# Self-attention's maxima: two key halves in two row halves of the array, one wait for both

## The chip, the cores and the metric

The program runs on one core of one Trainium2 chip, in one launch. The metric is the device time of that core in microseconds (us): the median of several runs. The engines of a core run their own instruction streams and wait for each other on semaphores: TensorE (PE in the profile; PEld is its weight load), VectorE (DVE), ScalarE (ACT), GpSimd (POOL), and SyncE (SP), which here issues the transfers.

## The reference, cut to what matters

Two transformer layers run over two sequences of 1024 tokens with 256 features. Each layer is self-attention, attention over 77 context rows, and a gated feed-forward. The change is in self-attention alone:

```python
h = _layernorm(x, ln1_g, ln1_b)
q = (h @ wq).reshape(B, S, 16, 64);  k, v likewise
attn = jnp.einsum('bihd,bjhd->bhij', q, k) * 64 ** -0.5
attn = jax.nn.softmax(attn, axis=-1)
x = jnp.einsum('bhij,bjhd->bihd', attn, v).reshape(B, S, 1024) @ wo + bo + x
```

A softmax may subtract any number from a row of scores before its exponentials, if it is the same for the whole row. The kernel subtracts something near the row's largest score, so that no exponential overflows. That number needs no great precision.

## The kernel before, in words

**Precision.** A 32-bit number is held as two 16-bit parts, an upper and a lower one, and a product is made of three 16-bit products (upper by upper, upper by lower, lower by upper; `three`, lines 892 to 896). The queries and keys of a pair of heads are made on TensorE into one bank of PSUM. ScalarE copies the upper part out (L1331), VectorE takes the rest (L1533, a step called *take*), and SyncE then spreads the four staged parts over the tiles `qa`, `qb`, `ka` and `kb` of the two heads, head by head (L620). A head has 64 features, so a tile of 128 rows holds two things: `qa` has the upper part of the queries in both halves of its rows, `ka` the upper part of the keys in the head's own half (`mine`) and their lower part in the other (`others`).

**Rounds, pairs, heads, steps.** There are four rounds (two layers by two sequences). A round's self-attention walks eight pairs of heads, two heads to a pair, eight steps to a head: 4 x 8 x 2 x 8 = 512 steps. Every engine walks the same list of steps, which `self_unit` writes out, and does its share of each; nothing reorders an engine's queue. TensorE's share of a step is, in this order:

1. the first key half of one tile of *maxima* (L980): 128 queries by 512 keys into PSUM, for the head that comes next;
2. what is *placed* in this step for the next pair: a projection of queries (`q`, two steps), of keys (`k`, two) or of values (`v`, two); or a `merge` (two, transposes), or one of the three small products for the context (`ck`, `cm`, `cv`). Some steps have none;
3. `score`: the scores of 512 queries and 256 keys (L997, L1004), for two exponentials of ScalarE (L1373, L1374);
4. the second key half of the tile of maxima (L980 again);
5. `value`: probabilities by values of an earlier step, 24 short products (L1022 to L1026).

VectorE's share is, in this order: the reduction of the first half of the maxima (L1574), the take of what was placed (L1533 for `q` and `k`, L1539 `v`, L1545 `merge`, L1549, L1555, L1564), the reduction of the second half, and then, where it falls to VectorE and not to GpSimd, the lower part of an earlier step's probabilities (*refine*, L1585), and at two steps of each head a reciprocal and a product (*gather*, L1591 and L1593).

**Counts.** In a round, 28 of the 128 steps have a projection of queries or keys placed and 14 one of values (seven pairs have a next one), 14 have a merge, and 8 each have `ck`, `cm` and `cv`. Over the four rounds that is 112, 56, 56, 32, 32 and 32; the other 192 steps have nothing placed. In the first pair of a round some steps hold two tiles of maxima, since that pair's own are not all made yet.

**The banks.** The maxima have two banks of PSUM, `work[0]` and `work[2]`, used in turn (`PEAK_RING` is 2). VectorE's reduction frees one by counting up `peak_free`, which starts at 2. `next_peak` makes product number n wait for n + 1, so for the reduction of number n - 2: a first half waits for the first half of the tile before it, a second half for the second.

Of the kernel before, what the change touches and what calls it, by code (L numbers as in the profile page):

```python
# [10 lines left out]
F16 = mybir.dt.float16  # L11
# [3 lines left out]
P = 128  # L15
# [3 lines left out]
HEADS, DH = 16, 64  # L19
# [8 lines left out]
BLK = 512  # L28
# [7 lines left out]
HALF = TILES // 2  # L36
# [94 lines left out]
PEAK = ("max",)  # L131
# [17 lines left out]

FIRST_POLISHED = (0, 1, 2, 3, 4, 5, 6)  # L150
SCORE_RING, PEAK_RING, HIGH_RING = 2, 2, 1
MOVES = 12


def queries(par, ahead):
# [220 lines left out]
def build(nc, io):  # L376
    ctx = ExitStack()
    with ctx:
        def sb(name, shape, dtype=F32):
            return ctx.enter_context(nc.sbuf_tensor(name, shape, dtype))  # L380
# [4 lines left out]
        def sem(name):  # L385
            return ctx.enter_context(nc.semaphore(name))
# [5 lines left out]
        self_peaks = [work[0], work[2]]  # L392
# [26 lines left out]
        xn = sb("xn", [P, 4, DIM])  # L419
# [21 lines left out]
        qa = [[sb(f"qa{p}{i}", [P, TOKENS], F16) for i in range(2)] for p in range(2)]  # L441
        qb = [[sb(f"qb{p}{i}", [P, TOKENS], F16) for i in range(2)] for p in range(2)]
        ka = [[sb(f"ka{p}{i}", [P, TOKENS], F16) for i in range(2)] for p in range(2)]
        kb = [[sb(f"kb{p}{i}", [P, TOKENS], F16) for i in range(2)] for p in range(2)]
        vals = [sb(f"vals{p}", [P, TILES, 2, VW], F16) for p in range(2)]
        prob32 = sb("prob32", [P, 4, TOKENS])
        prob = [sb(f"prob{i}", [P, 4, TOKENS], F16) for i in range(2)]
# [22 lines left out]
        def moves(which, par, head):  # L470

            mine, others = [slice(r, r + DH) for r in (head * DH, (1 - head) * DH)]
            up, low = [part[mine, :] for part in staged["qk".index(which)]]
            qa_, qb_, ka_, kb_ = [t[par][head] for t in (qa, qb, ka, kb)]
            if which == "q":
                return [(qa_[mine, :], up), (qa_[others, :], up), (qb_[mine, :], low)]
            return [(ka_[mine, :], up), (ka_[others, :], low), (kb_[mine, :], up)]

        def o_half(s):

# [49 lines left out]
        a = collections.namedtuple("Sems", names)(*[sem(f"self_{n}") for n in names.split()])  # L530
# [357 lines left out]
        def _(pe):  # L888
# [9 lines left out]
            def attention(g):  # L898
                pace = Pace(g)
                b = g % BATCH  # L900

                def bank():

                    n = pace.here(*HIGH)
                    if n >= len(first_high):
                        pe.wait_ge(a.work_free, pace.n(*HIGH) + HIGH_RING)
                    elif n >= 4:
                        pe.wait_ge(a.work_free, pace.n(*HIGH) - 3 + HIGH_RING)
                    elif n == 2 and g:

                        pe.wait_ge(inner_ready, g * (BLKS * FF_CHUNKS) + 2)
                    return high_bank(n)

                def next_peak():

                    pe.wait_ge(a.peak_free, pace.n(*PEAK) + 1)
                    return self_peaks[pace.here(*PEAK) % PEAK_RING]

                def weight(kind, c, column):
                    return [wp[kind][:, part, column + (c if column == 0 else 2 * c), :] for part in range(2)]  # L920

                def do(step, pair):
                    par, head, s = step.par, step.head, step.step
# [3 lines left out]
                    elif step.kind in ("q", "k"):  # L927
# [3 lines left out]
                        out = bank()  # L931
# [5 lines left out]
                    elif step.kind == "v":  # L937
                        out = bank()
# [7 lines left out]
                    elif step.kind == "ck":  # L946

                        pe.wait_ge(cross_split, pace.n("ck") + 1)
                        out = bank()
# [4 lines left out]
                    elif step.kind == "cm":  # L954

                        out = bank()
# [4 lines left out]
                    elif step.kind == "cv":  # L961
                        out = bank()
# [7 lines left out]
                    elif step.kind == "arrive":  # L970

                        pe.wait_ge(a.head0_ready, pace.n("arrive", times=8 * MOVES) + (8 * MOVES + CREDIT))
                    elif step.kind == "max":
                        if head == 1 and s == (0, 0):

                            pe.wait_ge(a.head1_ready, pace.n("arrive", times=8 * MOVES) + CREDIT)
                        out = next_peak()
                        t, h = s
                        first_query = t // HALF * BLK + t % HALF
                        pe.matmul(out[:, :], qa[par][head][:, first_query:first_query + (P - 1) * HALF + 1:HALF],  # L980
                                  ka[par][head][:, h * BLK:(h + 1) * BLK], start=True, stop=True)\
                            .then_inc(a.peak_full, 1)
                    elif step.kind == "score":
                        if pace.here("score") == 0:

# [6 lines left out]
                        out = scores[pace.here("score") % SCORE_RING]  # L992
# [3 lines left out]
                        for keys, at in parts:  # L996
                            pe.matmul(out[:, at], ka[par][head][:, keys], qa[par][head][:, q],  # L997
                                      start=True, stop=False)
# [8 lines left out]
                    elif step.kind == "value":  # L1007
# [7 lines left out]
                        for i, k in enumerate([2 * (s % KEY_STEPS) + i for i in range(2)]):  # L1015
                            v = vals[par][:, k, head, :]
                            for t in range(HALF):
                                out = self_outs[:, t * OUT_W:(t + 1) * OUT_W]
# [4 lines left out]
                                          stop=False, skip_group_check=True)  # L1023
# [3 lines left out]
                                                 stop=(k == TILES - 1), skip_group_check=True)  # L1027
                        last.then_inc(a.probs_used, 1)
                    elif step.kind == "merge":
                        out = bank()  # L1030
# [281 lines left out]
        def _(act):  # L1312
            act.sem_inc(a.exp_done, SCORE_RING)

            def attention(g):
# [7 lines left out]
                def do(step, pair):  # L1323
                    par, head, s = step.par, step.head, step.step
                    if step.kind == "start":

                        act.wait_ge(a.head0_ready, pace.pairs(8 * MOVES) + CREDIT)
                        act.wait_ge(a.head1_ready, pace.pairs(8 * MOVES) + CREDIT)
                    elif step.kind in ("q", "k"):
# [153 lines left out]
            for dest, source in moves("k", 0, 0):  # L1483
                act.dma_start(dest, source).then_inc(a.head0_ready, 16)
# [412 lines left out]
```

## Time and profile before

| what | us |
|---|---|
| median of 3 runs (2157.67 to 2160.73) | 2160.64 |
| the profiled execution, its own time | 2162.83 |
| its span, from the first to the last instruction | 2161.1 |

The span is what the profile's rows add up to; about 1.7 us lie around it. Busy time is the time in which an engine has at least one instruction under way. Matmuls are pipelined: one of 512 columns has a duration of 0.38 us, but the next one starts 0.22 us after it, so the distance of two starts tells what a matmul costs and not its duration.

### The profile page before, as it was taken

To read this page: it belongs to the slowest core of one execution; us is meant where nothing else is said; L and a number is where in the kernel's file an instruction comes from. 1 tells how busy PE (TensorE), PEld (TensorE's weight loads), DVE (VectorE), ACT (ScalarE), POOL (GpSimd) and SP (SyncE) were. 2 spreads that over 40 slices of the span, in tenths; PEclk is the share of its full clock that TensorE was granted. 3 is DMA by queue.
4 is the path that set the end of the run, shared out by engine and by line. 5 is a ranking of instruction groups with operands and counts; after the bars stand their busy time and mean duration, and the time that the engine had idled before them with its cause. 6 is when DMAs were issued, how large, how long until landed. Compare 5 with 4: busy or idle time off the path is not lost.

```text
span 2161.1 us, 58920 instructions
## 1 busy us (share of the span) xinstructions
PE 2087.5 (97%) x25120; PEld 1413.0 (65%) x25120; DVE 1618.5 (75%) x3014; ACT 1473.5 (68%) x1950; POOL 1375.3 (64%) x860
## 2 busy tenths in 40 slices
PE   6999999999999999999999999999999999999999
PEld 2666666775666666668466666676746666667675
DVE  6888887657688888765768888866577888885664
ACT  4888889345488888834548888874455888886442
POOL 6878887353378887835347887773424888775540
PEclk8999999999999999999999999999999999999999
DMA  4322220040332232004032233100403323210120
GB/s 137 77 56 65 72 73 19 11 96 26 77 92 65 56 84 61 19 16 99 25 94 75 65 77 77 45 29 9 97 21 90 85 72 83 56 39 21 23 62 20
DMA packets 134245, 127.82 MB, mean 59 GB/s; under 512 B 83424, under 2 KB 95712, under 8 KB 133984
## 3 DMA queue, kind: packets, MB, share of 16 engines
q1 hardware_dynamic: 133744, 123.67, 23.0%
q8 instruction: 198, 3.24, 0.6%
q14 instruction: 63, 0.52, 0.1%
q10 hardware_dynamic: 240, 0.39, 0.1%
HBM read 55.72 MB, written 4.19 MB: 28 GB/s over the span
## 4 chain that ended last, share of the span: by engine, by line
PE 74%; DVE 9%; ACT 5%; POOL 4%; issue 4%; DMA 2%; SPq 1%; POOLq 1%; DVEq 0%; ACTq 0%
PE work L980 10%; PE scores L1004 9%; PE scores L997 9%; PE scores L894 5%; PE scores L896 5%; PE scores L895 5%; PE work L1026 5%; PE work L1022 5%; PE work L1024 5%; PE work L894 4%; PE work L896 4%; PE work L895 4%; DVE minima L1574 2%; ACT prob L1374 1%; PE work L1034 1%
## 5 line engine op out<-in xcount | busy, mean ns | idle before, releaser
L830 POOL TENSOR_TENSOR prob<-prob 128x1024 f16<-128x1024 f32 x328 | 709.4, 2179 | 290.1 <-ACT prob L1374 274.4
L1574 DVE TENSOR_REDUCE minima<-work 128x1 f32<-128x512 f32 x1024 | 681.7, 683 | 53.3 <-PE work L980 47.2
L1373 ACT ACTIVATE prob<-scores 128x1024 f32<-128x1024 f32 x512 | 526.3, 1028 | 94.8 <-PE scores L1004 75.1
L1374 ACT ACTIVATE prob<-scores 128x1024 f16<-128x1024 f32 x512 | 522.8, 1021 | 0.0
L1022 PE MATMUL work<-vals,prob 128*128 128x65 f16 x4096 | 428.8, 192 | 2.2 <-POOL prob L830 1.8
L1026 PE MATMUL work<-vals,prob 128*128 128x65 f16 x4096 | 429.4, 195 | 0.0
L1024 PE MATMUL work<-vals,prob 128*128 128x64 f16 x4096 | 429.2, 193 | 0.0
L1022 PEld LDWEIGHTS work<-vals,prob 128*128 128x128 f16 x4096 | 383.0, 99 | 66.1 <-issue 17.9
L1024 PEld LDWEIGHTS work<-vals,prob 128*128 128x128 f16 x4096 | 379.8, 97 | 52.8
L980 PE MATMUL work<-ka,qa 128*128 128x512 f16 x1024 | 390.2, 384 | 24.6 <-DVE minima L1574 19.2
L1026 PEld LDWEIGHTS work<-vals,prob 128*128 128x128 f16 x4096 | 380.2, 97 | 0.0
L1004 PE MATMUL scores<-qb,kb 128*128 128x512 f16 (+1 forms) x1024 | 305.5, 379 | 0.0
L997 PE MATMUL scores<-qa,ka 128*128 128x512 f16 x1024 | 305.1, 380 | 0.3
L1585 DVE TENSOR_TENSOR prob<-prob 128x1024 f16<-128x1024 f32 x184 | 247.9, 1347 | 15.2 <-ACT prob L1374 15.2
L894 PE MATMUL scores<-wide,oT 128*128 128x256 f16 x768 | 210.9, 275 | 0.9 <-issue 0.5
L895 PE MATMUL scores<-wide,oT 128*128 128x256 f16 x768 | 211.0, 275 | 0.0
L896 PE MATMUL scores<-wide,oT 128*128 128x256 f16 x768 | 210.9, 275 | 0.0
L980 PEld LDWEIGHTS work<-ka,qa 128*128 128x128 f16 x1024 | 115.8, 113 | 107.0 <-DVE minima L1574 37.6
L1004 PEld LDWEIGHTS scores<-qb,kb 128*128 128x128 f16 (+1 forms) x1024 | 100.6, 98 | 121.2 <-issue 0.6
L894 PE MATMUL scores<-hT,wide 128*128 128x512 f16 (+1 forms) x416 | 158.9, 382 | 3.8 <-DVE prob L1780 3.6
L895 PE MATMUL scores<-hT,wide 128*128 128x512 f16 (+1 forms) x416 | 157.7, 379 | 0.0
L896 PE MATMUL scores<-hT,wide 128*128 128x512 f16 (+1 forms) x416 | 157.7, 379 | 0.0
(168 smaller groups left out, 4161.3 us busy)
## 6 DMA issues: line engine op xcount, KB each, us to landing
qa<-staged_q SPq DMA_DIRECT2D x128, 128.0 KB, 2.3
ka<-staged_k SPq DMA_DIRECT2D x126, 128.0 KB, 2.3
raw_even<-in_pairs SPq DMA_DIRECT2D x32, 384.0 KB, 3.4
raw_odd<-in_pairs SPq DMA_DIRECT2D x32, 384.0 KB, 3.4
raw_odd<-in_pieces SPq DMA_DIRECT2D x20, 512.0 KB, 3.4
raw_even<-in_pieces SPq DMA_DIRECT2D x20, 512.0 KB, 3.5
qb<-staged_q SPq DMA_DIRECT2D x64, 128.0 KB, 2.3
kb<-staged_k SPq DMA_DIRECT2D x63, 128.0 KB, 2.3
```

Source lines behind the costliest of these rows:

```text
L830: pool.tensor_tensor(prob[1][:, slot, :], prob32[:, slot, :], prob[0][:, slot, :], ALU.subtract).then_inc(a.polished, 1)
L894: pe.matmul(out, left[0], right[0], start=first, stop=False)
L895: pe.matmul(out, left[0], right[1], start=False, stop=False)
L896: return pe.matmul(out, left[1], right[0], start=False, stop=last)
L980: pe.matmul(out[:, :], qa[par][head][:, first_query:first_query + (P - 1) * HALF + 1:HALF], ka[par][head][:, h * BLK:(h + 1) * BLK], start ...
L1004: last = pe.matmul(out[:, at], kb[par][head][rows_, keys], qb[par][head][rows_, q], start=False, stop=True)
L1022: pe.matmul(out, p_hi, v[:, DH:VW], start=(first and i == 0 and t == 0), stop=False, skip_group_check=True)
L1024: pe.matmul(out[:, 0:DH], p_hi, v[:, 0:DH], start=False, stop=False, skip_group_check=True)
L1026: last = pe.matmul(out, p_lo, v[:, DH:VW], start=False, stop=(k == TILES - 1), skip_group_check=True)
L1373: act.activation(prob32[:, n % RING, :], source, ACT.Exp)
L1374: act.activation(prob[0][:, n % RING, :], source, ACT.Exp)\
L1574: dve.tensor_reduce(minima[:, t, h:h + 1], out[:, :], AX.X, ALU.max, negate=True)\
```

## The change

The two halves of a tile of maxima are multiplied in one place, where the first half stood, and from upper parts alone. The first half uses the 64 rows `mine` of `qa` and `ka`; the second uses the 64 rows `others` of `qa` (the same upper queries) and of a new tile `km`, which holds the upper part of the second 512 keys in those rows. Both wait once, for `n + 2`. `km` lies in the memory of `xn` and is filled by one more transfer for each head and pair (`MOVES` counts 14 in place of 12). In the steps' list nothing is moved: VectorE's two reductions stay where they are.

```diff
-MOVES = 12
+MOVES = 14
...
+        km = [xn[:, p, :].bitcast(F16) for p in range(2)]
...
-            return [(ka_[mine, :], up), (ka_[others, :], low), (kb_[mine, :], up)]
+            return [(ka_[mine, :], up), (km[par][others, :], up[:, BLK:2 * BLK]), (ka_[others, :], low),
+                    (kb_[mine, :], up)]
...
-                def next_peak():
-
-                    pe.wait_ge(a.peak_free, pace.n(*PEAK) + 1)
-                    return self_peaks[pace.here(*PEAK) % PEAK_RING]
-
...
-                        out = next_peak()
                         t, h = s
+                        if h:
+                            return
+                        n = pace.here(*PEAK)
+                        mine, others = [slice(r, r + DH) for r in (head * DH, (1 - head) * DH)]
                         first_query = t // HALF * BLK + t % HALF
-                        pe.matmul(out[:, :], qa[par][head][:, first_query:first_query + (P - 1) * HALF + 1:HALF],
-                                  ka[par][head][:, h * BLK:(h + 1) * BLK], start=True, stop=True)\
-                            .then_inc(a.peak_full, 1)
+                        queries_ = slice(first_query, first_query + (P - 1) * HALF + 1, HALF)
+
+                        pe.wait_ge(a.peak_free, pace.n(*PEAK) + 2)
+                        pe.matmul(self_peaks[n % PEAK_RING][:, :], qa[par][head][mine, queries_],
+                                  ka[par][head][mine, 0:BLK], start=True, stop=True).then_inc(a.peak_full, 1)
+                        pe.matmul(self_peaks[(n + 1) % PEAK_RING][:, :], qa[par][head][others, queries_],
+                                  km[par][others, :], start=True, stop=True).then_inc(a.peak_full, 1)
```

On TensorE, in a step of the first pair with a projection of queries placed (L894 to L896; `work0` and `work2` are the banks of the maxima, `scores0` the step's scores, `work3` the values), the row before is:

```order
L980 MATMUL work0<-ka11,qa11 128x512 [waits self_peak_free]
L894 MATMUL work1<-hT0,wpS 128x512 [waits self_work_free]
L895 MATMUL work1<-hT1,wpS 128x512
L896 MATMUL work1<-hT0,wpS 128x512
...
L997 MATMUL scores0<-qa10,ka10 128x512 [waits self_exp_done]
...
L1004 MATMUL scores0<-qb10,kb10 128x512 x2
L980 MATMUL work2<-ka11,qa11 128x512 [waits self_peak_free]
L1022 MATMUL work3<-vals0,prob0 128x65 [waits self_polished]
```

and now, with the line numbers of the changed kernel (L983 and L985 are the two halves, L896 to L898 the projection, L1001 and L1008 the scores, L1026 the values):

```order
L983 MATMUL work0<-ka11,qa11 128x512 [waits self_peak_free]
L985 MATMUL work2<-xn,qa11 128x512
L896 MATMUL work1<-hT0,wpS 128x512 [waits self_work_free]
L897 MATMUL work1<-hT1,wpS 128x512
L898 MATMUL work1<-hT0,wpS 128x512
...
L1001 MATMUL scores0<-qa10,ka10 128x512 [waits self_exp_done]
...
L1008 MATMUL scores0<-qb10,kb10 128x512 x2
L1026 MATMUL work3<-vals0,prob0 128x65 [waits self_polished]
```

The second half has moved from behind the scores to right behind the first, and its wait has gone into the first one's.

On VectorE, around a take of keys (L1537) and one of `ck` (L1553) in the first pair, the changed kernel's order is the following; before, the same rows stand in the same order, four line numbers lower:

```order
L1578 TENSOR_REDUCE minima<-work0 128x1 [waits self_peak_full]
L1537 SCALAR_TENSOR_TENSOR staged_k1<-work1,staged_k0 128x512 [waits self_work_high]
L1578 TENSOR_REDUCE minima<-work2 128x1 [waits self_peak_full]
L1578 TENSOR_REDUCE minima<-work0 128x1 [waits self_peak_full]
L1553 SCALAR_TENSOR_TENSOR kd1<-work1,kd0 64x77 [waits self_work_high]
```

Nothing moved here: the reduction of `work2` stands behind the take.

On SyncE, in the first spread of keys, the row before is:

```order
L643 DMA qb01<-shift160 1x128x4
L620 DMA ka10<-staged_k0 64x1024
L620 DMA ka10<-staged_k1 64x1024
L620 DMA kb10<-staged_k0 64x1024
L620 DMA ka11<-staged_k0 64x1024
```

and now:

```order
L645 DMA qb01<-shift160 1x128x4
L622 DMA ka10<-staged_k0 64x1024
L622 DMA xn<-staged_k0 64x512
L622 DMA ka10<-staged_k1 64x1024
L622 DMA kb10<-staged_k0 64x1024
L622 DMA ka11<-staged_k0 64x1024
```

One transfer more stands in each head's share, ahead of the other head's.

## Rows read from the trace of the kernel before

**Rows 1.** The page, part 1: busy us (share of the span) and instructions.
```profile
PE 2087.5 (97%) x25120; PEld 1413.0 (65%) x25120; DVE 1618.5 (75%) x3014; ACT 1473.5 (68%) x1950; POOL 1375.3 (64%) x860
```

**Rows 2.** Self-attention of round one: length, busy of PE, PEld, DVE, ACT, POOL; clock.
```profile
41.00:378.00 337.00, 330.73 (x4478) 219.06 (x4477) 280.65 (x487) 287.11 (x357) 264.86 (x140) 1.00 0.24 62
```

**Rows 3.** Groups by line (page, part 5): busy us, mean ns, idle before, its releaser.
```profile
L980 PE MATMUL work<-ka,qa 128*128 128x512 f16 x1024 | 390.2, 384 | 24.6 <-DVE minima L1574 19.2
```

**Rows 4.** Timeline of PE, a step with a projection of queries: start us, duration us.
```profile
666.70 0.38 PE L980 MATMUL work<-ka,qa 128*128 128x512 f16 x1
666.92 0.38 PE L894 MATMUL work<-hT,wpS 128*128 128x512 f16 x1
...
668.21 0.59 PE L997 MATMUL scores<-qa,ka 128*128 128x512 f16 x2
...
669.08 0.38 PE L980 MATMUL work<-ka,qa 128*128 128x512 f16 x1
...
670.04 0.38 PE L980 MATMUL work<-ka,qa 128*128 128x512 f16 x1
```

**Rows 5.** Timeline of ACT and DVE in the same step: copy, take, second reduction.
```profile
668.41 0.60 ACT L1331 ACTIVATE staged_q<-work 128x512 f16<-128x512 f32 x1 [0.54 <-PE work L896]
...
669.04 0.69 DVE L1533 SCALAR_TENSOR_TENSOR staged_q<-work,staged_q 128x512 f16<-128x512 f32 x1 [1.23 <-ACT staged_q L1331]
669.65 0.68 DVE L1574 TENSOR_REDUCE minima<-work 128x1 f32<-128x512 f32 x1
```

**Rows 6.** Timeline of DVE and PE where PE waits for a reduction.
```profile
318.89 0.68 DVE L1574 TENSOR_REDUCE minima<-work 128x1 f32<-128x512 f32 x1
...
319.62 0.41 PE L980 MATMUL work<-ka,qa 128*128 128x512 f16 x1 [0.66 <-DVE minima L1574]
```

**Rows 7.** Timeline of PE around the eight transposes with 8 weight columns.
```profile
435.03 0.38 PE L896 MATMUL scores<-hT,wide 128*124 128x512 f16 x1
435.34 0.61 PE L1107 MATMUL work<-ident,x_shift 128*8 128x128 f16 x8
435.88 0.43 PE L894 MATMUL scores<-hT,wide 128*124 128x512 f16 x1
436.15 0.38 PE L895 MATMUL scores<-hT,wide 128*124 128x512 f16 x1
```

**Rows 8.** Groups by line: the take of values.
```profile
L1539 DVE SCALAR_TENSOR_TENSOR vals<-work,vals 128x512 f16<-128x512 f32 x64 | 44.3, 694 | 41.3 <-ACT vals L1339 41.3
```

**Rows 9.** Timeline, a step with a merge: PE's tile, its second reduction, the next tile.
```profile
658.73 0.38 PE L980 MATMUL work<-ka,qa 128*128 128x512 f16 x1
...
661.04 0.68 DVE L1574 TENSOR_REDUCE minima<-work 128x1 f32<-128x512 f32 x1
...
661.21 0.38 PE L980 MATMUL work<-ka,qa 128*128 128x512 f16 x1
```

**Rows 10.** Timeline, a step with `cm`: the same three.
```profile
683.02 0.38 PE L980 MATMUL work<-ka,qa 128*128 128x512 f16 x1
...
684.94 0.68 DVE L1574 TENSOR_REDUCE minima<-work 128x1 f32<-128x512 f32 x1
...
685.45 0.38 PE L980 MATMUL work<-ka,qa 128*128 128x512 f16 x1
```

**Rows 11.** Timeline, a step with nothing placed: two tiles' starts, two reductions at once, one alone.
```profile
673.38 0.38 PE L980 MATMUL work<-ka,qa 128*128 128x512 f16 x1
...
674.33 1.28 DVE L1574 TENSOR_REDUCE minima<-work 128x1 f32<-128x512 f32 x2
...
675.41 0.38 PE L980 MATMUL work<-ka,qa 128*128 128x512 f16 x1
...
675.82 0.69 DVE L1574 TENSOR_REDUCE minima<-work 128x1 f32<-128x512 f32 x1 [0.22 <-PE work L980]
```

**Rows 12.** Timeline, VectorE's refine, and SyncE issuing two transfers of keys.
```profile
670.25 1.39 DVE L1585 TENSOR_TENSOR prob<-prob 128x1024 f16<-128x1024 f32 x1
...
680.33 1.24 SPq L620 DMA_DIRECT2D ka<-staged_k  x2
```

## The prediction

> **What bounds the kernel now.** I read the busy shares first: TensorE is busy 97% of the span, the others 75% or less [rows 1]; in the first round's self-attention, 337 us long, TensorE has 331 us, ScalarE 287, VectorE 281 and GpSimd 265, at a granted clock of 1.00, the 2.4 GHz level [rows 2]. So TensorE is the bound and three engines stand close behind it. Then the groups by line: the 1024 products of maxima waited 24.6 us in all [rows 3], so before the change the reductions hardly ever hold TensorE up. Then the timeline of one step with a projection of queries, which the rest is built on [rows 4]. Products start 0.22 us after each other (666.70 to 666.92). The step runs from 666.70 to the next tile's first half at 670.04, 3.34 us without a hole: 0.22 the first half, 1.29 the projection (666.92 to 668.21), 0.87 the scores (to 669.08), 0.96 the second half and the values.
>
> The timeline of ScalarE and VectorE beside it decides this case [rows 5]. ScalarE copies the projection from 668.41, VectorE's take follows at 669.04, and only behind the take comes the second reduction, 669.65 to 670.33. The next tile has by then been started at 670.04, 0.29 us earlier. That is allowed now, because a first half waits for the first reduction alone.
>
> **What goes and what comes.** The pair of products costs 0.43 us a tile now. Two at once would cost one product and a small shift. With 512 tiles that is the gain to be had: 512 x (0.43 - 0.24) = 97 us, if nothing else came.
>
> *The switch between whole rows and half rows.* No row before shows a product of 64 rows. The nearest rows are the eight transposes with 8 weight columns, which use another part of the array than their neighbours [rows 7]. Ahead of them the next start is due at 435.03 + 0.22 = 435.25 and comes at 435.34: 0.09 us lost. Behind them, eight starts 0.055 us apart end at 435.78 and the next comes at 435.88: 0.10 lost, and its weight load, which could not be made beforehand, costs 0.05 more (436.15 - 435.88 is 0.27, not 0.22). With 128 weight columns the uncovered load is 0.03: where TensorE waited for a reduction, the product's duration is 0.41 and not 0.38 [rows 6]. The price of a switch is thus between 0 (a product can't start before the one ahead has been fed in, so it gains nothing) and 0.15 us; I take 0.09 each way with 0.03 for a load, the rows' own value. A tile then costs 0.09 + 0.03 (first load) + 0.03 (second load, by which the second half starts later) + 0.21 + 0.09 + 0.03 = 0.48 us against 0.43, so by itself the change loses 0.05 x 512 = 28 us. The Trainium skill has a rule for this in "TensorEngine Tiling (Array Packing)", Key Properties: changing the tiling mode, not just the tile, drains the engine. Those transposes agree with it at 0.09 us; for 64 rows no run here shows it.
>
> *The wait.* It is the dearer part. Both halves now wait for both reductions of the tile before, and the second of them stands behind the take in VectorE's queue. So in a step with something placed a ring closes: tile, projection, copy, take, second reduction, next tile. Nothing behind the waiting product on TensorE (projection, scores, values) can go ahead. Its length for a projection: from the end of the second reduction to the next product 0.05 (318.89 + 0.68 = 319.57, then 319.62 [rows 6]); loads 0.06; the product 0.21; the switch back with a load 0.12. That makes 0.44 to the projection's start; the switch on entry is hidden in the wait. From there the trace has 666.92 to 670.33, 3.41. The ring is 3.85 us against 3.34: 0.51 a step. Put for any step: from the first half's start to the end of the second reduction, less 0.22, plus 0.44.
>
> - Projections of queries and keys 112, of values 56 (their take lasts 0.69 too [rows 8]): 168 x 0.51 = 86.
> - Merges: 658.73 to 661.72 is 2.99, plus 0.22 makes 3.21, against 2.48 now (661.21) [rows 9]: 0.73 x 56 = 41.
> - `cm`: 683.02 to 685.62 is 2.60, makes 2.82 against 2.43 [rows 10]: 0.39 x 32 = 12.
> - `ck` and `cv` are of the same build with two and three small pieces to a take: I set them between the last two, 0.56 x 64 = 36.
> - Nothing placed, 192 steps. A step takes 2.03 (673.38 to 675.41). After a reduction's end VectorE needs 0.05 + 0.03 + 0.41 (from a product's start to its reduction, 675.41 to 675.82) + 1.28 for two reductions in a row [rows 11] = 1.77, less than TensorE's 2.03 + 0.05, so the switch alone counts. But where a refine, 1.39 us [rows 12], comes first (by the list of steps about one such step in five), the two reductions end some 0.45 later than TensorE's own work. 0.8 x 0.05 + 0.2 x 0.45 = 0.13; x 192 = 25.
> - The first pair's steps that carry two tiles pass the ring with two more reductions behind the take: three to a round, about 0.5 more each, 6.
> - The transfers: SyncE issues two in 1.24 us [rows 12], so each head's keys arrive 0.64 us later. Within a round steps with slack follow the spread; at a round's start, where TensorE comes directly to the maxima, 0.64 x 4 = 3.
>
> What hides the rest: the exponentials, 2.05 us a step, get more room, since steps become longer. The lower parts left out of the maxima change the shift a little and no time. The sum is 86 + 41 + 12 + 36 + 25 + 6 + 3 = 209. The profiled execution took 2162.8 (span 2161.1 and 1.7 around it), 2.2 above the median of the runs. 2162.8 + 209 = 2372, against the median 2370.
>
> **Rivals.**
>
> *The halves one after the other.* The two products have their own weights, rows and banks, but no row here shows two at once. Run in turn, a tile costs 0.21 - 0.03 = 0.18 more, in the ring too: 512 x 0.18 = 92, so 2462.
>
> *The ring stays open, the switch is paid.* If the second reduction ended before TensorE comes back (a quicker copy and take, VectorE being otherwise free), only 28 us remain: 2188. Against it: copy, take and reduction follow each other within 0.04 us in the step shown [rows 5]; nothing in them waits for anything that the change speeds up.
>
> *Faster.* The place is the 512 tiles, the price 0.19 us each, the mechanism two products in the time of one. It decides if a switch costs under 0.06 us both ways together and the reductions are done when TensorE comes back. Both would give 2161 - 97 = 2064 at most; ScalarE, at 287 of 337 us [rows 2], still fits. For it: TensorE's share and the unbroken pitch of 0.22. Against it: the 0.29 us by which the second reduction is already late, and rows 7. With free switches and the ring as it stands, the ring is still 3.76 against 3.34. The Trainium skill's "TensorE: Matmul & The Clock Gate", Part 3, The mechanism, states that products in different row groups overlap, their starts about 4 ns apart. By that rule alone the time is this rival's; the trace has no such pair.
>
> **How the numbers follow.** The ring with halves at once 0.83, halves in turn 0.07, open ring with switches 0.05, faster 0.04, no change (a switch that costs just what the overlap gives, open ring) 0.01. The likeliest is the first: 2370. Its own bounds are the switch's: with none, 320 steps with something placed lose 0.09 less (29) and 192 others up to 0.26 less (50), so 2291; with 0.05 more for every load's exposure on the way out, 512 x 0.02 to 0.04, 2390. Upwards the range has to reach the halves in turn, 2462. So 2290 to 2465. About 0.2%, 4 us, is what a measurement can tell from no change. Faster 0.04, same 0.01, slower 0.95.
>
> **What would show it.** In the profile after: waits of the first half (L983) for VectorE's reductions near 200 us in place of 25; TensorE's share near 85%; a step with a projection near 3.85 us and a merge near 3.2; the second half (L985) starting about 0.03 us after the first, and the next product about 0.3 after that. A start 0.21 later would show halves in turn; a next product 0.22 after the second half would show a free switch. I am wrong at the root if the first half finds both reductions done in steps with a projection, so that those steps stay at 3.34 or fall below.

## The result, and the profile after

The changed kernel took 2335.95 us (median of four runs, 2332.85 to 2338.72) against 2159.66 for the kernel before (2157.67 to 2160.73): a ratio of 1.0816, 95% interval 1.0799 to 1.0833. It is 176 us slower; 2370 was forecast, in a range of 2290 to 2465. The profiled execution took 2334.5, with a span of 2332.8.

Part 1 of the page after, in the form of [rows 1]:

```profile
PE 2108.8 (90%) x25120; PEld 1388.7 (60%) x25120; DVE 1644.1 (70%) x3014; ACT 1480.5 (63%) x1950; POOL 1350.6 (58%) x860
```

Nearly the same busy time lies in a span that is 172 us longer; every engine's share has fallen. The first round's self-attention, to set against [rows 2]:

```profile
42.40:421.80 379.40, 336.79 (x4478) 214.40 (x4477) 286.21 (x486) 288.74 (x357) 258.36 (x140) 0.99 0.23 57
```

It takes 379.4 us in place of 337.0, at a mean granted clock of 0.99 in place of 1.00 (for this 0.01 see "The rest" below). TensorE is busy for 337 us of it, so it now stands still for over 40. For what, the groups by line tell (L983 and L985 are the two halves, L1578 their reduction), to set against [rows 3]:

```profile
L1578 DVE TENSOR_REDUCE minima<-work 128x1 f32<-128x512 f32 x1024 | 681.3, 683 | 116.0 <-PE work L985 114.2
...
L983 PE MATMUL work<-ka,qa 64*128 64x512 f16 x512 | 207.8, 406 | 180.3 <-DVE minima L1578 173.2
...
L985 PE MATMUL work<-xn,qa 64*128 64x512 f16 x512 | 208.7, 408 | 0.0
```

The first half waited 173 us for reductions, where 19 were waited before; the second half never waits. And the reductions in turn waited 114 us for L985: that is the mark of a ring, two engines that wait for each other by turns. Part 4 of the page, the chain that ended last, first before, then after:

```profile
PE 74%; DVE 9%; ACT 5%; POOL 4%; issue 4%; DMA 2%; SPq 1%; POOLq 1%; DVEq 0%; ACTq 0%
```

```profile
PE 43%; DVE 32%; ACT 11%; issue 7%; POOL 4%; DMA 1%; POOLq 1%; SPq 0%; ACTq 0%; DVEq 0%
```

TensorE set the end for three quarters of the time; now VectorE and ScalarE set it for 43%.

One step with a projection of queries shows the ring. The timeline of PE, to set against [rows 4] (start us, duration us; in brackets the idle time before and its releaser):

```profile
722.25 0.41 PE L983 MATMUL work<-ka,qa 64*128 64x512 f16 x1 [0.62 <-DVE minima L1578]
722.25 0.40 PE L985 MATMUL work<-xn,qa 64*128 64x512 f16 x1
722.59 0.39 PE L896 MATMUL work<-hT,wpS 128*128 128x512 f16 x1
722.82 0.38 PE L897 MATMUL work<-hT,wpS 128*128 128x512 f16 x1
...
726.07 0.40 PE L983 MATMUL work<-ka,qa 64*128 64x512 f16 x1 [0.41 <-DVE minima L1578]
```

Its weight loads:

```profile
722.25 0.11 PEld L983 LDWEIGHTS work<-ka,qa 64*128 64x128 f16 x1 [0.74 <-DVE minima L1578]
722.25 0.11 PEld L985 LDWEIGHTS work<-xn,qa 64*128 64x128 f16 x1
722.59 0.10 PEld L896 LDWEIGHTS work<-hT,wpS 128*128 128x128 f16 x1 [0.23 <-issue]
```

And ScalarE's copy, VectorE's take and second reduction, to set against [rows 5]:

```profile
724.09 0.60 ACT L1335 ACTIVATE staged_q<-work 128x512 f16<-128x512 f32 x1 [1.24 <-PE work L898]
...
724.72 0.69 DVE L1537 SCALAR_TENSOR_TENSOR staged_q<-work,staged_q 128x512 f16<-128x512 f32 x1 [1.34 <-ACT staged_q L1335]
725.33 0.68 DVE L1578 TENSOR_REDUCE minima<-work 128x1 f32<-128x512 f32 x1
```

The two halves truly run at once: both products start at 722.25 and both loads too (3 ns apart in the trace's nanoseconds). The next product comes 0.34 later. But the second reduction ends at 725.33 + 0.68 = 726.01, and only then, at 726.07, may the next tile start: the step is 3.82 us and was 3.34. Copy, take and reduction follow each other without a hole, VectorE having stood idle for 1.34 before the take.

All steps, from one tile's first product to the next one's (medians; loss is the sum of all differences to before; the first steps of a round and the steps between rounds apart):

| step | number | before | after | loss, us |
|---|---|---|---|---|
| projection q, k | 100 | 3.340 | 3.821 | 56.5 |
| projection v | 56 | 3.387 | 3.874 | 27.2 |
| merge | 48 | 2.476 | 3.094 | 27.6 |
| `ck` | 28 | 2.242 | 2.851 | 10.3 |
| `cm` | 28 | 2.429 | 2.796 | 10.5 |
| `cv` | 28 | 2.767 | 3.354 | 16.2 |
| nothing placed | 156 | 2.076 | 2.052 | 3.0 |
| first steps of rounds | 48 | 1.727 | 1.902 | 12.9 |

With 1.5 in the last steps of rounds and between rounds that is 166 of the span's 172. The other 5.6 lie in four intervals that the table leaves out, one a round: behind the last step that holds two tiles, the next tile waits for a second reduction that stands behind VectorE's gather (L1595, L1597), 2.67 us where it was 1.25. Of the 100 steps with q or k, 98 start the next tile within 0.08 us of the second reduction's end; before the change none had to.

### The profile page after: what moved, and what is told of

Its sections match the earlier page's. It is cut to its first block, busy times and chain, and to the rows that moved or that the text cites. A ratio compares the mean times of both kernels' runs of the same rounds, so it can differ in the third digit from the quotient of the medians.

```text
span 2332.8 us, 58984 instructions
## 1 busy us (share of the span) xinstructions
PE 2108.8 (90%) x25120; PEld 1388.7 (60%) x25120; DVE 1644.1 (70%) x3014; ACT 1480.5 (63%) x1950; POOL 1350.6 (58%) x860
## 4 chain that ended last, share of the span: by engine, by line
PE 43%; DVE 32%; ACT 11%; issue 7%; POOL 4%; DMA 1%; POOLq 1%; SPq 0%; ACTq 0%; DVEq 0%
DVE minima L1578 14%; PE work L983 6%; DVE prob L1589 6%; PE scores L896 5%; PE scores L898 5%; PE scores L897 5%; PE work L896 4%; PE work L898 4%; PE work L897 3%; PE scores L1001 3%; PE scores L1008 2%; ACT prob L1377 2%; ACT prob L1378 2%; DVE vals L1543 2%; DVE staged_q L1537 2%
## 5 line engine op out<-in xcount | busy, mean ns | idle before, releaser
L832 POOL TENSOR_TENSOR prob<-prob 128x1024 f16<-128x1024 f32 x328 | 724.2, 2213 | 470.1 <-ACT prob L1378 462.6
L1578 DVE TENSOR_REDUCE minima<-work 128x1 f32<-128x512 f32 x1024 | 681.3, 683 | 116.0 <-PE work L985 114.2
L1026 PE MATMUL work<-vals,prob 128*128 128x65 f16 x4096 | 431.6, 193 | 0.4
L1026 PEld LDWEIGHTS work<-vals,prob 128*128 128x128 f16 x4096 | 383.3, 99 | 63.5 <-issue 6.0
L983 PE MATMUL work<-ka,qa 64*128 64x512 f16 x512 | 207.8, 406 | 180.3 <-DVE minima L1578 173.2
L1001 PE MATMUL scores<-qa,ka 128*128 128x512 f16 x1024 | 309.1, 384 | 0.5
L1008 PE MATMUL scores<-qb,kb 128*128 128x512 f16 (+1 forms) x1024 | 306.2, 380 | 0.0
L1589 DVE TENSOR_TENSOR prob<-prob 128x1024 f16<-128x1024 f32 x184 | 268.0, 1456 | 15.0 <-ACT prob L1378 15.0
L896 PE MATMUL scores<-wide,oT 128*128 128x256 f16 x768 | 209.4, 273 | 0.8 <-issue 0.8
L898 PE MATMUL scores<-wide,oT 128*128 128x256 f16 x768 | 209.3, 273 | 0.0
L985 PE MATMUL work<-xn,qa 64*128 64x512 f16 x512 | 208.7, 408 | 0.0
L983 PEld LDWEIGHTS work<-ka,qa 64*128 64x128 f16 x512 | 56.0, 109 | 245.6 <-DVE minima L1578 197.3
L1008 PEld LDWEIGHTS scores<-qb,kb 128*128 128x128 f16 (+1 forms) x1024 | 101.1, 99 | 122.7 <-issue 3.0
L896 PE MATMUL scores<-hT,wide 128*128 128x512 f16 (+1 forms) x416 | 158.9, 382 | 3.8 <-DVE prob L1784 3.6
L897 PE MATMUL scores<-hT,wide 128*128 128x512 f16 (+1 forms) x416 | 157.7, 379 | 0.0
```

Of the source, the lines that this page charges most:

```text
L832: pool.tensor_tensor(prob[1][:, slot, :], prob32[:, slot, :], prob[0][:, slot, :], ALU.subtract).then_inc(a.polished, 1)
L896: pe.matmul(out, left[0], right[0], start=first, stop=False)
L897: pe.matmul(out, left[0], right[1], start=False, stop=False)
L898: return pe.matmul(out, left[1], right[0], start=False, stop=last)
L1008: last = pe.matmul(out[:, at], kb[par][head][rows_, keys], qb[par][head][rows_, q], start=False, stop=True)
L1026: pe.matmul(out, p_hi, v[:, DH:VW], start=(first and i == 0 and t == 0), stop=False, skip_group_check=True)
```

## The experiments

Each ran on the chip beside the kernel before, which took 2159.5 to 2161.7 us there; ratios have their 95% intervals.

**Both reductions ahead of the take.** The list of steps gives VectorE the second reduction directly behind the first; on TensorE nothing is moved.

```diff
-        out += [step for step in peaks_of[s] if step.kind == "arrive"] + peaks[:1]
+        out += [step for step in peaks_of[s] if step.kind == "arrive"] + peaks[:2]
...
-        spread = [peaks[1:2], peaks[2:3], peaks[3:]] if len(peaks) > 2 else [[], peaks[1:], []]
+        spread = [[], peaks[2:], []]
```

> The changed kernel with one edit in the list of steps: VectorE's second reduction stands ahead of the take of what is placed, right behind the first reduction. Theory (ring: the next tile waits for a second reduction that stands behind the take): the ring opens, a tile then costs 0.447 us on TensorE (0.098 in, 0.004, 0.336 to the next product, 0.011) against 0.432 before, so 2161 + 0.015 x 512 = 2168; bounds 2150 to 2185. Rival (the switch to half rows and back is what costs): nothing of that is changed, so about 2336.

Measured: 2206.29 (2203.35 to 2209.97), ratio 1.0215 (1.0198 to 1.0232). Timeline of PE, then of DVE, in a step with a projection of queries:

```profile
680.64 0.41 PE L983 MATMUL work<-ka,qa 64*128 64x512 f16 x1
...
683.99 0.40 PE L983 MATMUL work<-ka,qa 64*128 64x512 f16 x1
```

```profile
681.09 1.29 DVE L1578 TENSOR_REDUCE minima<-work 128x1 f32<-128x512 f32 x2 [0.55 <-PE work L985]
683.12 0.69 DVE L1537 SCALAR_TENSOR_TENSOR staged_q<-work,staged_q 128x512 f16<-128x512 f32 x1 [0.74 <-ACT staged_q L1335]
```

The reductions are through at 682.38, 1.6 us before the next tile needs their banks. The step is 3.35 long, and no projection step waits any more. So at least 130 of the 176 us were the ring through VectorE's queue (the new order costs something itself, as the third experiment shows). The time is 21 above the upper bound I had set: of the 46 us left, the first steps of rounds have 13, nothing placed 8, merges 6.5, `cv` 6, `ck` 4, projections 2.5, and the four intervals left out above 2.5. In half of the merges VectorE has a refine of the step before in front of the two reductions:

```profile
710.27 1.71 DVE L1589 TENSOR_TENSOR prob<-prob 128x1024 f16<-128x1024 f32 x1
711.90 1.27 DVE L1578 TENSOR_REDUCE minima<-work 128x1 f32<-128x512 f32 x2
```

That step's tile starts at 710.52 and the next at 713.23, 0.06 after the reductions' end (711.90 + 1.27 = 713.17): a short ring in place of the long one.

**Whole rows, one wait.** The kernel before, with its 128-row products, both halves in one place behind one wait for n + 2; 12 transfers as before.

```diff
-                        out = next_peak()
...
+                        if h:
+                            return
+                        n = pace.here(*PEAK)
...
+                        pe.wait_ge(a.peak_free, pace.n(*PEAK) + 2)
+                        for i in range(2):
+                            pe.matmul(self_peaks[(n + i) % PEAK_RING][:, :], qa[par][head][:, queries_],
+                                      ka[par][head][:, i * BLK:(i + 1) * BLK], start=True, stop=True)\
+                                .then_inc(a.peak_full, 1)
```

> The kernel before with both halves in one place and one wait for both reductions, but with products over all 128 rows as before and without the new tile or its transfer; VectorE's order as in both kernels. Theory (ring): the ring stays closed and holds 0.432 + 0.03 for the two products in place of 0.346 + 0.011, so 0.1 more in about 320 steps: 2336 + 33 = 2369; bounds 2345 to 2385. Rival (switch): without half rows the time goes back to about 2161.

Measured: 2349.02 (2348.24 to 2350.02), ratio 1.0876 (1.0859 to 1.0892). PE and DVE in a step with a projection:

```profile
721.60 0.60 PE L986 MATMUL work<-ka,qa 128*128 128x512 f16 x2
722.03 0.38 PE L894 MATMUL work<-hT,wpS 128*128 128x512 f16 x1
...
725.58 0.41 PE L986 MATMUL work<-ka,qa 128*128 128x512 f16 x1 [0.48 <-DVE minima L1580]
```

```profile
724.85 0.68 DVE L1580 TENSOR_REDUCE minima<-work 128x1 f32<-128x512 f32 x1
```

With no half rows at all nearly the whole loss is there, with the same wait for the second reduction (725.53 to 725.58). So the switch of the array's form is not needed for the loss. The half rows even make the ring shorter, by 0.11 a projection step (3.929 here).

**Whole rows, both reductions ahead of the take.** The edit of the first experiment on the kernel before.

> The kernel before with both halves in one place (each with its own wait, all 128 rows) and both reductions ahead of the take. Theory (ring): no ring, TensorE streams as before: 2145 to 2165, and the difference from the same order with half rows is the net price of halves at once, some 7 us in favour of whole rows (0.015 x 512). Rival (switch): 2161 too; it would put the difference from half rows at 170 or more.

Measured: 2179.95 (2179.02 to 2181.10), ratio 1.0093 (1.0078 to 1.0108): a miss by 15. Of its 20 us the `cv` steps have 12 (median 3.260, before 2.767); projections stay at 3.34. The order by itself is not free. What makes `cv` long stands in the waits of the weight loads, first before, then here:

```profile
PEld work L894 <- DVE oT L1545: 4.9, 5, 1.1
```

```profile
PEld work L894 <- DVE oT L1545: 15.8, 28, 1.1
```

What is placed has one bank, which the take (here a merge's, L1545) frees; the take now stands behind a refine and both reductions, and the next placed product waits for it. The order opens one ring and closes another, shorter one.

The half rows cost 26 beyond it (2206 to 2180), where I had expected about 7: 5 of them are the transfers (next). The other 21 were not taken apart; they hold the switch, and a fall of the clock in the first pair (see "The rest" below).

**The transfers alone.** The kernel before with `km` and its two transfers a pair, never read.

```diff
-MOVES = 12
+MOVES = 14
...
+        km = [xn[:, p, :].bitcast(F16) for p in range(2)]
```

> The kernel before with the new tile and its transfers alone (14 moves a pair; the tile is filled and never read). Theory (ring): the transfers are covered but for a round's start: 0 to 5 us more than before, 2161 to 2166. Rival (the transfers cost a good part of the loss, through SyncE's queue): 2180 or more.

Measured: 2164.61 (ten runs, 2162.33 to 2168.14), ratio 1.0023 (1.0014 to 1.0033): 5 us. The weight loads' waits for the keys' transfers doubled, from 6.3 us, 6 times, to:

```profile
PEld work L982 <- DMA kb<-staged_k: 13.1, 12, 5.2
```

**Half rows, each in its old place with its own wait.** Two stays in half rows a tile, and nothing at once.

```diff
-                        if h:
-                            return
...
+                        rows_, keys_ = (others, km[par][others, :]) if h else (mine, ka[par][head][mine, 0:BLK])
-                        pe.wait_ge(a.peak_free, pace.n(*PEAK) + 2)
+                        pe.wait_ge(a.peak_free, pace.n(*PEAK) + 1)
```

> The changed kernel's products (64 rows, upper parts, the new tile and its transfer) in the old places and with the old waits: each half by itself, the second behind the scores. Theory (ring for the time lost, and a switch that the overlap just pays): the ring is open again, but each half now pays the way in and out by itself, 0.098 + 0.336 + 0.011 = 0.445 us against 0.216, so 2161 + 5 for the transfers + 0.23 x 1024 = 2400; some of it falls into waits that TensorE has anyway: 2370 to 2405. Rival (half rows cost nothing to enter and leave; only the shared wait costs): 2165.

Measured: 2359.24 (2358.92 to 2369.12) against 2161.65, ratio 1.0929 (1.0905 to 1.0953). The waits of weight loads, and where the load could not go ahead (us, times, longest):

```profile
PEld work L982 <- issue: 147.8, 349, 1.1
PEld work L1023 <- issue: 107.7, 470, 0.6
...
PEld work L982 <- DVE minima L1575: 87.3, 190, 1.3
```

Here the switch can be priced by itself: from the last whole-row product to the first of half rows 0.10 us is lost, on the way back 0.12 (sums over the pairs of lines at the values, L1027 to L982 less a pitch of 0.030, and L982 to L1023 less 0.216: 45.9 us in 460, 55.9 us in 464). A step with nothing placed has two stays and takes 2.48 in place of 2.08. So with each half by itself the kernel loses 198 us, more than the changed kernel's 176; part of that is waits for reductions (87.3 above, 37.6 at L980 before). The time is 11 below my bounds and 41 below the 2400 of the working; that this part of the switch fell into waits that TensorE has anyway, as the expectation put it, was not measured.

**Both halves in the same 64 rows**, one after the other behind the common wait (`MOVES` 12).

```diff
-                        pe.matmul(self_peaks[(n + 1) % PEAK_RING][:, :], qa[par][head][others, queries_],
-                                  km[par][others, :], start=True, stop=True).then_inc(a.peak_full, 1)
+                        pe.matmul(self_peaks[(n + 1) % PEAK_RING][:, :], qa[par][head][mine, queries_],
+                                  ka[par][head][mine, BLK:2 * BLK], start=True, stop=True).then_inc(a.peak_full, 1)
```

> The changed kernel with the second half multiplied in the same 64 rows as the first (the head's own rows of the keys), so that the two cannot run at once; without the new tile and its transfers, else the same. Theory (the two halves run at once and that is worth one product's 0.213 us in every tile, in the ring too): 2336 - 5 + 0.213 x 512 = 2440; bounds 2420 to 2450. Rival (they do not really run at once; the records of their starts mislead): 2331, as the changed kernel without its transfers.

Measured: 2426.09 (2421.18 to 2427.62), ratio 1.1224 (1.1207 to 1.1241). PE at a tile:

```profile
762.75 0.40 PE L983 MATMUL work<-ka,qa 64*128 64x512 f16 x1 [0.40 <-DVE minima L1578]
762.99 0.38 PE L985 MATMUL work<-ka,qa 64*128 64x512 f16 x1
763.30 0.39 PE L1001 MATMUL scores<-qa,ka 128*128 128x512 f16 x1
```

The second half starts 0.24 later and the next product 0.55 after the first, in place of 0.34. Different rows are what lets the halves run at once, and that is worth 90 us here.

**The wait split.** The first half waits for n + 1, the second for n + 2.

```diff
-                        pe.wait_ge(a.peak_free, pace.n(*PEAK) + 2)
+                        pe.wait_ge(a.peak_free, pace.n(*PEAK) + 1)
...
+                        pe.wait_ge(a.peak_free, pace.n(*PEAK) + 2)
```

> The changed kernel with the wait parted: the first half waits for the first reduction of the tile before, the second half, right behind it, for the second. Theory (what counts is where the second reduction stands on VectorE, behind the take): TensorE stands at the second half in place of the first, the ring stays closed: 2336, bounds 2320 to 2350. Rival (the single wait of both halves is the fault): back to about 2165 to 2200.

Measured: 2323.01 (2322.64 to 2326.64), ratio 1.0754 (1.0738 to 1.0770). The wait has moved to the second half (L986):

```profile
PEld work L986 <- DVE minima L1579: 138.5, 348, 1.3
```

Counted from one second half to the next, the steps are as long as in the changed kernel: 3.817 us with `q` or `k` placed and 3.871 with `v`, for 3.821 and 3.874 (medians). It is not the common wait by itself that costs, but that the second half stands ahead of the placed work: what stands behind it on TensorE can't pass.

**The refines moved.** Three tries to give the first experiment, or the kernel before, other steps in which VectorE makes the lower parts (`POLISHED`, the steps of each head that go to GpSimd): in the first no refine stands ahead of a merge's reductions any more; in the other two only the second heads of a pair change. VectorE makes what the list does not name: in first heads of a pair 0, 3 and 7 (the expectation below says 1, 3 and 7), in second heads 0, 2 and 6.

```diff
-POLISHED = ((1, 2, 4, 5, 6), (1, 3, 4, 5, 7))
+POLISHED = ((1, 3, 4, 5, 6), (0, 2, 3, 4, 5))
```

> The kernel with both reductions ahead of the take (2206), with VectorE's three refines of a head moved to steps that a projection follows: steps 1, 3 and 7 done by VectorE in even heads become 0, 2 and 7, those of odd heads 1, 6 and 7. Theory (what is left there is a refine of 1.2 to 1.5 us between a tile and its reductions where the next step is short: merge 0.23, cv 0.26, a step with nothing placed 0.12): 18 less, 2188; bounds 2175 to 2200. Rival (what is left is the price of half rows): 2206.

Measured: 2229.19 (2225.25 to 2233.25), ratio 1.0316 (1.0295 to 1.0337). A miss: merges wait no more, but the projections of queries and keys lost 37 us, since VectorE comes late behind two refines in a row (the second step with `q` takes 0.72 us longer).

```diff
-POLISHED = ((1, 2, 4, 5, 6), (1, 3, 4, 5, 7))
+POLISHED = ((1, 2, 4, 5, 6), (0, 2, 4, 5, 7))
```

> The kernel with both reductions ahead of the take (2206), with VectorE's refines of odd heads alone moved: 1, 3 and 6 in place of 0, 2 and 6, so that none stands between a take of values and a merge; even heads stay. Theory (the 46 us left over before are 5 of transfers, some 6 of the switch, 13 of the first steps of a round and about 16 of refines ahead of a merge): 2206 - 16 = 2190; bounds 2183 to 2198. Rival (moving refines only shifts the wait to GpSimd or to the projections, as the move of six refines did): 2206 or more.

Measured: 2251.99 (2245.47 to 2254.77) against 2160.26, ratio 1.0420 (1.0400 to 1.0440). A miss: the `cv` steps lost 38 us (median 4.231). DVE and POOL there:

```profile
732.00 3.08 DVE L1589 TENSOR_TENSOR prob<-prob 128x1024 f16<-128x1024 f32 x1
```

```profile
731.87 5.19 POOL L832 TENSOR_TENSOR prob<-prob 128x1024 f16<-128x1024 f32 x2 [0.19 <-issue]
```

The refine took 3.08 us beside GpSimd's work of the same kind, and in the 24 `cv` steps that have one 2.93 on average; the mean of the 184 is 1.80 in this run and 1.35 before. The next tile waits for the two reductions behind it. The same list of steps on the kernel before:

> The kernel before with the same refines moved in odd heads (1, 3 and 6), and nothing of the change. Theory (before, TensorE hardly waits for reductions, 25 us at L980 in all): 0 to 8 us less, 2152 to 2161. Rival (the placing of refines matters as much there as in the kernel with both reductions first): 16 less, 2145.

Measured: 2181.00 (2178.37 to 2182.87), ratio 1.0099 (1.0082 to 1.0116). The miss is of the same cause: `cv` steps at 3.576, 24 us, with refines of 2.27 on average in them. So no kernel run here beats the one before, and moving the refines costs the kernel before 21 us too.

## Why the prediction was right, and by what it was off

**The bound moved as foretold.** The ring of tile, projection, copy, take, second reduction and next tile closed in every kind of step that has something placed. The first experiment opened it by the order of VectorE's queue alone and got 130 us back; whole rows in the same place closed it as well.

**The length of the ring.** From the projection's start to the end of the second reduction 722.59 to 726.01 is 3.42 us, against 3.41 in the working. The other part was 0.44 and measures 0.40: 0.06 from the reduction to the tile (0.05 and a load's 0.03 were taken), and 0.34 from there to the projection, where I had the second load behind the first; the loads go at once. Over 156 projections the mean loss is 0.54 a step (83.7 us) for 0.51; without the four in the first pairs, which lost 5.9, it is 0.51.

**Merges were mis-sized**: 0.73 foretold, 0.575 measured (27.6 over 48). The term that failed is the way around the ring on the other engines. The way from the transposes to the end of the second reduction was 2.77 in [rows 9], 658.95 to 661.72. After, it is 2.61: 713.40 to 716.01, from these rows of PE and DVE:

```profile
713.06 0.40 PE L983 MATMUL work<-ka,qa 64*128 64x512 f16 x1 [0.51 <-DVE minima L1578]
...
713.40 0.66 PE L1038 MATMUL work<-ident,o_nat 128*128 128x128 f32 x4
...
716.16 0.38 PE L983 MATMUL work<-ka,qa 64*128 64x512 f16 x1 [0.49 <-DVE minima L1578]
```

```profile
715.33 0.68 DVE L1578 TENSOR_REDUCE minima<-work 128x1 f32<-128x512 f32 x1
```

What had become quicker is seen on ACT, before and after:

```profile
658.89 1.02 ACT L1374 ACTIVATE prob<-scores 128x1024 f16<-128x1024 f32 x1
659.80 0.60 ACT L1344 ACTIVATE oT<-work 128x512 f16<-128x512 f32 x1
```

```profile
714.09 0.60 ACT L1348 ACTIVATE oT<-work 128x512 f16<-128x512 f32 x1 [0.31 <-PE work L1038]
```

Before, the copy stood behind an exponential and came 0.85 after the transposes' start; after, ScalarE is idle and it comes 0.69 after (so in all 48 merges). I had written that the exponentials get more room, and had not asked what that gives to the ring, whose rows I took from a busy ScalarE.

**Nothing placed was mis-sized most**: 0.13 a step foretold, 0.02 measured (3.0 us over 156). Two things failed. An unblocked tile was put at 0.48 us and costs 0.446, against 0.432 before: 0.098 on entry (0.128 from a product of the values to the first half, less their pitch of 0.030) and 0.011 after the 0.336, so both switches are paid out of the overlap. And refines held up 44 of the 156 steps, which lost 6.7 us together (28 of them went from 2.107 to 2.329), where a fifth by 0.45, 14 us, was foretold. The other 112, for which 0.05 each was foretold, became 3.7 us shorter together; why, was not taken apart.

**The rest.** `cm` 0.375 a step for 0.39, `ck` and `cv` 0.47 for 0.56. The working put one tile into each of 512 steps, but by the list of steps the eight steps of a round's last head have none and the first pair's first head has thirteen: so 48 merges lose and not 56. What was forecast for the first steps, the starts of rounds and the transfers is 32 us of the 209 (the counts of the working less those of the table above) and 20 measured; the transfers by themselves are 5 and not 3. The sum by kind: projections 4 more than foretold, merges 8 less, `ck` and `cv` 5 less, nothing placed 17 less, the rest 12 less, together 38 of 209. One slip of the working stands outside the forecast: 0.05 x 512 is 26 and not 28, so the open ring with the switch paid was 2186.

A term that the working did not have is the clock. The stretch from the first projection of keys in a round's first pair to the end of that head, before in round three, then after in rounds two and three (length, busy times, granted clock; 1.00 is the 2.4 GHz level):

```profile
1114.00:1131.80 17.80, 16.68 (x187) 9.72 (x188) 14.58 (x29) 13.16 (x17) 12.19 (x7) 1.00 0.56 134
```

```profile
626.30:647.60 21.30, 16.45 (x186) 8.80 (x187) 14.86 (x28) 12.53 (x17) 12.77 (x6) 1.00 0.48 117
1199.50:1224.70 25.20, 20.91 (x186) 10.25 (x187) 15.01 (x28) 12.53 (x17) 12.76 (x6) 0.80 0.40 99
```

After, the clock is at the 1.2 GHz level for part of this stretch in rounds one, three and four (0.86, 0.80 and 0.80; before it was 1.00 in each), and these are 2.5, 3.9 and 3.9 longer than round two: about 10 of the 176 us. Ahead of it TensorE stands still for reductions between the two tiles of a step, which makes the way from one tile to the other 0.5 to 0.6 longer; it does so in round two as well, where the clock stayed up, so what decides is not shown. That the total came within 34 us of the forecast is thus in part luck: the forecast was too long in most kinds of step, and this loss, which it did not have, filled some of that.

**The rivals.** Halves in turn: refuted by starts 3 ns apart, and tried in the same rows (2426). The Trainium skill's "TensorE: Matmul & The Clock Gate", Part 3, The mechanism, has products in different row groups start about 4 ns apart; this trace agrees. Open ring: the first experiment is that rival made, but it stands at 2206 and not 2188: the order that opens it makes short rings elsewhere, and the first pairs lose as above. Faster: with the switch a pair costs 0.446 against 0.432 for two products in turn, so the switch takes all that the overlap gives. The Trainium skill's "TensorEngine Tiling (Array Packing)", Key Properties, says that a change of the tiling mode drains the engine; the half rows apart agree that a switch costs time, with 0.10 us in and 0.12 out.

**The marks.** The waits of L983, near 200 foretold in place of 25, came to 180 us in the count that [rows 3] gives as 24.6; the waits of its weight loads for reductions came to 197:

```profile
PEld work L983 <- DVE minima L1578: 197.3, 332, 1.9
```

TensorE's share came to 90% and not 85%: the span is shorter than forecast, and a product's recorded duration reaches into the wait behind it.

**Left open.** Of the 13 us that the first steps of rounds lose in the first experiment, some go with the clock: there the stretch above takes 19.7 us at 1.00 in round two and 22.1 at 0.85 in rounds three and four. The others were not taken apart. Several tiles in one stay in half rows, so that one switch serves more products, was not tried: the banks of the maxima hold one tile.

## What to carry to other kernels

Before two instructions are put in one place, write down for each where its releaser stands in the other engine's queue: the later one sets both, and if work that it needs is queued behind the waiting instruction, a ring closes whose length, not the engine's work, is the step. Packing small products into parts of the array pays only as far as the overlap exceeds the switch in and out, so price a stay, not a product. And take a ring's pieces from rows with idle neighbours: a copy that stood behind other work will not stand there when steps get longer.

## What the runs showed of the hardware that was not expected

- Products in two row halves start 3 ns apart, and so do their weight loads; a pair takes 0.336 us to the next product, where one 64-row product behind another in the same rows makes it 0.55.
- A stay in half rows costs 0.10 us on entry even where nothing is waited for (the half rows apart), and 0.12 on the way out: the 0.336 from the second half to the next product, less the 0.216 from one whole-row product to the next.
- VectorE's refine with two inputs took 1.21 to 1.23 us, all 89 of them, where GpSimd had nothing under way in the run with the refines of second heads moved, and up to 3.09 where GpSimd's instruction had started first; the 3.08 is one of these, and the 1.39 in [rows 12] ran beside GpSimd too. In the kernel before, the 59 refines that started ahead of the GpSimd instruction beside them all took 1.21 to 1.22: a refine that starts first is not slowed there. The Trainium skill's "SBUF — State Buffer", Who interferes with whom, says that a VectorE instruction with two inputs in SBUF contends with a GpSimd instruction that reads there; the run agrees.
